# Attention and mixture-of-experts layer: in cross-only steps TensorE turns probabilities before x, and the output projection stands ahead of q

## What is computed

```python
def _L0_xattn_ref(queries, keys, values, Wq, bq, Wk, bk, Wv, bv, Wo, bo):
    q = (queries @ Wq + bq).reshape(B, L, H, dk)
    k = (keys @ Wk + bk).reshape(B, S, H, dk)
    v = (values @ Wv + bv).reshape(B, S, H, dk)
    scores = jnp.einsum('blhd,bshd->bhls', q, k)
    scores = jnp.where(causal[None, None], -jnp.inf, scores)
    attn = jax.nn.softmax(scores * scale, axis=-1)
    out = jnp.einsum('bhls,bshd->blhd', attn, v).reshape(B, L, H * dk)
    return out @ Wo + bo

x = x + _L0_xattn_ref(_layernorm(x, axis=-1), ctx_1024, ctx_1024, ...)
x = x + _L0_ffn_ref(_layernorm(x, axis=-1), ...)
```

## Time and profile before

| What | us |
|---|---|
| Median of three executions | 1707.7 |
| The profiled execution | 1707.36 |
| Its span | 1705.6 |
| Cross-only steps | 0 to 216 |
| Steps 14 to 51, routing, experts | 216 to the end |
| PE busy in the span | 1526.3 (89%) |
| DVE, ACT, POOL busy | 959.7, 688.9, 779.4 |
| xc load, median from issue to landing | 3.0 |

### The profile page before, as it was taken

How to read it: one execution, slowest core, us unless ns; L and a number is a source line. 1 busy time by engine, 2 the same in 40 slices (tenths; PEclk the granted TensorE clock), 3 DMA queues, 4 the chain that set the end, 5 groups by cost and what they waited for, 6 DMA issues and landing times. The chain is left out here.

```text
span 1705.6 us, 30593 instructions
## 1 busy us (share of the span) xinstructions
PE 1526.3 (89%) x11078; PEld 1332.6 (78%) x11079; DVE 959.7 (56%) x1691; ACT 688.9 (40%) x1359; POOL 779.4 (46%) x792
## 2 busy tenths in 40 slices
PE   4798888999999999999815899999999979999986
PEld 3566667888888888888714889899899869899975
DVE  2576555777777776777558535452333454443361
ACT  1234343555555555455320535343333444333341
POOL 1243334555555546565332546654343565463342
PEclk9999988999999999999958899999999989999999
DMA  6011121122122212111131334433332443342221
GB/s 233 22 56 51 63 70 43 63 71 74 66 71 66 79 58 69 68 64 61 48 110 36 90 68 93 101 94 87 71 91 39 99 111 81 79 106 59 35 39 22
DMA packets 62910, 124.09 MB, mean 73 GB/s; under 512 B 13456, under 2 KB 14128, under 8 KB 61865
## 3 DMA queue, kind: packets, MB, share of 16 engines
q1 hardware_dynamic: 44512, 92.41, 16.4%
q0 software_dynamic: 17920, 29.08, 9.8%
q10 hardware_dynamic: 328, 0.50, 0.1%
HBM read 88.69 MB, written 46.14 MB: 79 GB/s over the span
## 5 line engine op out<-in xcount | busy, mean ns | idle before, releaser
L1279 PE MATMUL hidden_ps<-gT,w 128*128 128x256 f32 x2880 | 352.4, 284 | 5.7 <-ACT hT L1201 2.2
L1279 PEld LDWEIGHTS hidden_ps<-gT,w 128*128 128x128 f32 x2880 | 350.0, 192 | 9.5 <-ACT hT L1201 4.9
L1308 PE MATMUL expert_ps<-w,hT 128*128 128x512 f32 x1440 | 340.6, 396 | 8.0 <-DVE og L1248 8.0
L1308 PEld LDWEIGHTS expert_ps<-w,hT 128*128 128x128 f32 x1440 | 272.6, 191 | 64.6 <-DVE og L1248 8.5
L1226 DVE TENSOR_TENSOR hT<-gl,hT 128x512 fp32r<-128x512 f32 x160 | 131.9, 833 | 247.4 <-ACT hT L1201 241.2
L1087 POOL TENSOR_TENSOR w<-raw,w 128x1024 fp32r<-128x1024 f32 x64 | 154.6, 2429 | 222.7 <-ACT w L1081 221.6
L1199 ACT ACTIVATE gl<-hidden_ps 128x512 f32<-128x512 f32 x160 | 95.6, 597 | 337.0 <-PE hidden_ps L1279 205.8
L1181 POOL DMA_INDIRECT out_dram<-og,idx x80 | 132.2, 1653 | 155.7 <-DVE og L1248 142.1
L1248 DVE TENSOR_SCALAR og<-expert_ps,shares 128x512 f32<-128x512 f32 x80 | 59.1, 749 | 162.6 <-PE expert_ps L1308 152.0
L1209 ACT ACTIVATE gT<-yk 128x256 fp32r<-128x256 f32 x160 | 66.9, 418 | 140.1 <-DVE yk L1235 138.1
L636 DVE TENSOR_TENSOR x<-main_ps,xc 128x512 f32<-128x512 f32 x32 | 22.1, 692 | 153.9 <-PE main_ps L315 153.9
(11 more groups left out here) (173 smaller groups left out, 3141.3 us busy)
## 6 DMA issues: line engine op xcount, KB each, us to landing
raw<-L_ffn_moe_w_dram SPq DMA_DIRECT2D x64, 512.0 KB
xa<-x_dram SPq DMA_DIRECT2D x32, 256.0 KB, 2.6
xc<-x_dram SPq DMA_DIRECT2D x32, 256.0 KB, 3.0
attended_rows<-x SPq DMA_DIRECT2D x32, 256.0 KB, 2.0
fx<-attended_rows SPq DMA_DIRECT2D x128, 64.0 KB
normed_tokens<-h SPq DMA_DIRECT2D x128, 64.0 KB
out_dram<-fx SPq DMA_DIRECT2D x128, 64.0 KB
fx<-qkv_rows_dram SPq DMA_DIRECT2D x1, 1536.0 KB, 6.4
```

The costliest lines, as they stand in the source:

```text
L1279: last = pe.matmul(pH[:, q, f * W:(f + 1) * W], w1[p][l][:, k, cols], xT[g.s % 2][r][:, k, :], start=k == 0 and n == 0, stop=k == KT - 1 a ...
L1308: last = pe.matmul(pY[:, k, :], hT[par][l][:, f, k * P:(k + 1) * P], w2[p][r][:, f, :], start=f == 0 and n == 0, stop=f == FT - 1 and n == 2)
```

## The change

In steps below FF TensorE turns the probabilities first, then x, then does the output projection, and q after it; psum_jobs lists them so; ScalarE copies xT_hi behind the four pT, and so in step 1 behind the token copies and wo_hi. From step 14 on the order is as before. VectorE, GpSimd and SyncE are not touched.

```diff
--- before.py
+++ after.py
@@ -158,10 +158,15 @@
     tx, tq, tp, tw = tile(i, 1), tile(i, 2), tile(i, LP), tile(i, LP + 1)
     fz, fq, fs, fo, ft, fr = (tile(i, FF + n) for n in range(6))
     free = 1 if i < FF else 0
-    jobs = [("xt", tx, 0, free)] + [("pt", tp, j, free) for j in range(4)] + [("p2t", fo, 0, 0), ("zt", fz, 0, 0)]
+    jobs = [("xt", tx, 0, free)] + [("pt", tp, j, free) for j in range(4)]
+    if free:
+        jobs = jobs[1:] + jobs[:1] + [("wo", tw, 0, free)]
+    jobs += [("p2t", fo, 0, 0), ("zt", fz, 0, 0)]
     if i % 2 == 0:
         jobs += [("q", tq, 0, 0), ("q", tq, 1, 0)]
-    jobs += [("wo", tw, 0, free), ("s2", fs, 0, 1), ("o2", fo, 0, 1), ("s", tq, 0, 0), ("qkv", fq, 0, 1),
+    if not free:
+        jobs += [("wo", tw, 0, free)]
+    jobs += [("s2", fs, 0, 1), ("o2", fo, 0, 1), ("s", tq, 0, 0), ("qkv", fq, 0, 1),
              ("lg", fr, 0, 1), ("qkv", fq, 1, 1)]
     if tq is not None and tq < S:
         jobs += [("val", tq, 0, 1)]
@@ -472,7 +477,7 @@
             act.activation(wq[0][:, :, :], rq, ACT.Copy).then_inc(s["wq_hi"], 1)
             for i in range(STEPS):
                 t = tile(i, 1)
-                if t is not None:
+                if t is not None and i >= FF:
                     act.wait_ge(s["xt_mm"], t + 1)
                     need(act, s["q_mm"], 2 * (t // 2))
                     act.activation(xT[0][:, :, (t % 2) * P:(t % 2 + 1) * P], parts(bank("xt", t)), ACT.Copy)\
@@ -491,6 +496,12 @@
                         act.activation(pT[:, j, :, :],
                                        bank("pt", t, j)[0:SK, :].rearrange("p (g n) -> p g n", g=4),
                                        ACT.Copy).then_inc(s["pt_evac"], 1)
+                t = tile(i, 1)
+                if t is not None and i < FF:
+                    act.wait_ge(s["xt_mm"], t + 1)
+                    need(act, s["q_mm"], 2 * (t // 2))
+                    act.activation(xT[0][:, :, (t % 2) * P:(t % 2 + 1) * P], parts(bank("xt", t)), ACT.Copy)\
+                        .then_inc(s["xt_hi"], 1)
                 f = tile(i, FF + 3)
                 if f is not None:
                     act.wait_ge(s["p2t_mm"], f + 1)
@@ -734,6 +745,25 @@
                     last = pe.transpose(bank(kind, t)[:, k * P:(k + 1) * P], src[:, k * P:(k + 1) * P], ident)
                 return last
 
+            def turn_x(tx):
+                pe.wait_ge(s["normed_x"], tx + 1)
+                transposes("xt", tx, xa[:, tx % 3, :]).then_inc(s["xt_mm"], 1)
+
+            def turn_probabilities(tp):
+                for b in range(4):
+                    pe.wait_ge(s["shared"], 2 * tp + b // 2 + 1)
+                    bank_free(pe, "pt", tp, b)
+                    for g in range(4):
+                        last = pe.transpose(bank("pt", tp, b)[0:SK, g * P:(g + 1) * P], pr[:, tp % 2, b, g, :],
+                                            ident)
+                    last.then_inc(s["pt_mm"], 1)
+
+            def project_out(tw):
+                pe.wait_ge(s["o_lo"], tw + 1)
+                bank_free(pe, "wo", tw)
+                split_matmuls(pe, bank("wo", tw), lambda h, k: oT[h][:, k, :], lambda h, k: wo[h][:, k, :])\
+                    .then_inc(s["wo_mm"], 1)
+
             pe.wait_ge(ctx_in, 16)
             pe.wait_ge(wk_in, 16)
             for n in range(8):
@@ -746,17 +776,14 @@
             for i in range(STEPS):
                 tx, tq, tp, tw = tile(i, 1), tile(i, 2), tile(i, LP), tile(i, LP + 1)
                 fz, fq, fs, fo, ft, fr = (tile(i, FF + n) for n in range(6))
-                if tx is not None:
-                    pe.wait_ge(s["normed_x"], tx + 1)
-                    transposes("xt", tx, xa[:, tx % 3, :]).then_inc(s["xt_mm"], 1)
+                if tx is not None and i >= FF:
+                    turn_x(tx)
                 if tp is not None:
-                    for b in range(4):
-                        pe.wait_ge(s["shared"], 2 * tp + b // 2 + 1)
-                        bank_free(pe, "pt", tp, b)
-                        for g in range(4):
-                            last = pe.transpose(bank("pt", tp, b)[0:SK, g * P:(g + 1) * P], pr[:, tp % 2, b, g, :],
-                                                ident)
-                        last.then_inc(s["pt_mm"], 1)
+                    turn_probabilities(tp)
+                if tx is not None and i < FF:
+                    turn_x(tx)
+                if tw is not None and i < FF:
+                    project_out(tw)
                 if fo is not None:
                     pe.wait_ge(s["shared2"], fo + 1)
                     transposes("p2t", fo, p2.rearrange("p b k -> p (b k)")).then_inc(s["p2t_mm"], 1)
@@ -773,11 +800,8 @@
                             last = split_matmuls(pe, bank("q", tq, j)[:, m * 256:(m + 1) * 256],
                                                  lambda h, k: wq[h][:, k, cols], lambda h, k: xT[h][:, k, :])
                         last.then_inc(s["q_mm"], 1)
-                if tw is not None:
-                    pe.wait_ge(s["o_lo"], tw + 1)
-                    bank_free(pe, "wo", tw)
-                    split_matmuls(pe, bank("wo", tw), lambda h, k: oT[h][:, k, :], lambda h, k: wo[h][:, k, :])\
-                        .then_inc(s["wo_mm"], 1)
+                if tw is not None and i >= FF:
+                    project_out(tw)
                 if fs is not None:
                     pe.wait_ge(s["q_turned"], fs + 1)
                     pe.wait_ge(s["k_turned"], fs + 1)
```

## The result

The changed kernel takes **1722.1 us** (median of 4 runs, 1719.5 to 1724.9) against 1708.3 (4 runs of the kernel before beside it): a ratio of 1.008, 95% interval 1.0062 to 1.0098. It is slower by 13.8 us; the forecast was 1718.0, in a range of 1710 to 1723.

A forecast was written before the change was run, and what follows sets the result against it. It took VectorE to bound odd steps and TensorE even steps in the first 216 us. Terms -5.5 + 1.45 + 6.7 + 3.7 + 2.6 + 1.9 = +10.8 on the kernel before gave 1718 us, range 1710 to 1723.

The forecast's parts named there:

- (a): Start, step 1: wo_hi no longer waits behind tile 0's transpose copy; tile 1's norm and all after gain 5.5 us.
- The collision: Start: VectorE's wq_lo and GpSimd's wo_lo meet at 22.7 us; if wo_lo waits it ends near 29, price 0.
- (b): Step 4: xT_hi waits behind four pT copies, q starts at 72.8 instead of 71.34: +1.45 us, perhaps 0.8 more.
- (c): Odd steps 5 to 13: xT_hi 2.22 us late delays VectorE's chain to mask: +6.7 us, +3.7 in 11 and 13.
- (d): Even steps 6 to 12: the copy of q, no longer covered by wo, delays the scores: +2.6 us together.
- (e): TensorE's clock in even steps: longer idle time brings two slow episodes of four, +1.9 us; range none to 7.2.
- rival B: Slower still: a low clock in every even step and a longer one in step 4; 1724 us, chance 0.09.
- A: Faster: ScalarE's order costs nothing, odd steps end on TensorE, the mask following scores, not norm_x; 1699 us, chance 0.11.
- C: About even: the odd steps' delay is half the forecast's, with no slow clock; 1711 us, chance 0.07.
- D: The start does not gain because wo_hi waits for something later than the landing at 20.6; 1724 us, chance 0.03.

The follow-up runs named there:

- version 1: The kernel before with only ScalarE's copy of tile 0's transpose moved behind wo_hi in step 1: 1706.6 us, ratio 0.9987.
- version 3: The changed kernel with q ahead of the output projection again, the rest as changed: 1728.4 us, ratio 1.0122.
- version 4: The changed kernel with filler matmuls in TensorE's idle stretch at the head of steps 6, 8, 10 and 12: 1714.1 us, ratio 1.0034.
- version 5: version 1 with VectorE's norm_x moved behind the subtraction of the row maxima in steps 1 to 13: 1698.3 us, ratio 0.993.
- version 2: version 1 with the output projection ahead of q in cross-only steps, x still turned first: 1708.7 us, ratio 0.9999.
- version 6: The changed kernel with xT_lo behind the exponential sums and statistics of x in steps 5, 7, 9, 11 and 13: 1705.9 us, ratio 0.9974.
- version 7: version 6 with norm_x also moved behind the subtraction of the row maxima in steps 1 to 13: 1699.3 us, ratio 0.9935.
- version 11: The kernel before with only norm_x moved behind the subtraction of the row maxima in steps 1 to 13: 1704.0 us, ratio 0.9987.

## Why the prediction came out as it did

**(a) The start, right.** -5.07 against -5.5, by the path described; counted from the start of wq_lo, which came 0.34 us later in this execution (22.63 against 22.29), it is -5.41. I took nothing for the clock at the start; q to scores took 8.31 us instead of 8.68 there, 0.37 back. The collision was seen; I had wo_lo end "near 29" if it had to wait, and it ended at 29.3. The Trainium skill, "SBUF — State Buffer", section "SBUF: two separate sides", has the port pair as an exclusive lock held by the first to start; wo_lo's 6.17 us beside an undisturbed wq_lo of 2.28 agrees. Waiting wq_lo out (1.78 us, to 24.91) and then taking 4.50 would make 6.28. The other order occurred too: in versions 1, 3, 4 and 5 wo_lo started first, kept 4.5 us, and it was wq_lo that took 6.1 to 6.4; in version 2 the two started within 0.02 us of each other and wq_lo kept its time. In version 1:

```profile
22.44 4.52 POOL L416 TENSOR_TENSOR wo_lo<-pr,wo_hi 128x2048 fp32r<-128x2048 f32 x1 [8.07 <-ACT wo_hi L485]
```

```profile
22.71 6.40 DVE L602 TENSOR_TENSOR wq_lo<-fx,wq_hi 128x2048 fp32r<-128x2048 f32 x1
```

The price is 0 either way: the first q comes 14.55 us behind wq_lo's start in the changed kernel and 14.54 in version 1.

**(b) Step 4, right in size, half for another reason.** +1.47 against +1.45. Locally q came only 0.71 later (71.34 - 5.07 to 66.98); the other 0.76 is q to scores at a low clock (8.61 us instead of 7.85), which I had named as an "up to 0.8 more" and not counted. Version 1, which has only the start, is slow for longer in step 4 as well (9.18 us).

**(c) Odd steps, right.** 1.92 us each against 2.22 in steps 5, 7 and 9, and 2.45 and 2.50 against 1.84 and 1.85 in 11 and 13: +10.7 against +10.4, of which 0.5 in each of 11 and 13 is not there in version 4. I put that down to the clock; in step 11 its slow stretch is shorter there (184 to 188 us against 183 to 190), for step 13 it is not shown. The 2.22 was 0.3 too large because I took the four copies at the 2.24 us of the earlier trace rows, where the fourth waited for its quarter. With all quarters turned in time xT_hi starts 1.91 us after the first copy. Version 6 shows the chain by taking its head away; version 2, whose steps 5, 7 and 9 do not change, shows that wo's place has no part in it.

**(d) Even steps at full clock, right.** +0.51, +0.56, +0.57 and +1.20 in version 4, against 0.52, 0.57, 0.50 and 0.98. The bare copy of q is worth 1.14 to 1.22 by version 2; half of it comes back because the last quarter no longer waits for xT_lo.

**(e) The clock, mis-sized.** This is the one term that failed. I took two episodes of four at 0.96, +1.9; measured were four of four, 7.0 us in steps 6 to 12. In steps 6, 8, 10 and 12 the last quarter to the scores took 12.01, 11.57, 13.07 and 13.13 us, where the forecast's own sum at full clock (0.78 + 2.89 + 6.89 from step 12's) is 10.6. I gave "2.81 us of idle time in step 12 did not bring it down" as evidence against. That gap was the exception of four: in the same trace the gaps of 3.53 us in step 4 and of 2.68 in steps 11 and 13 were followed by 0.50. I had the slow wo of 11 and 13 in part (c) and the slow step 4 in part (b), and drew nothing from them for the clock. The gaps then became 3.18 and 5.73, as I had worked out myself ("about 3", "near 4.7").

So what happened is rival B's mechanism (1724, with a chance of 0.09 that was too low): a low clock in all four even steps and a longer one in step 4. That the time still fell inside my range is in part luck. I had written that what the first 216 us lose is carried to the end; 2.7 us came back late, in the drain. With them the profiled execution would have stood at 1724.4, above the 1723 where I had ended the range. What comes back is not a constant either: version 4 is 10.0 us late at step 13 and 5.2 in its span.

Sum as measured: -5.1 + 1.5 + 10.7 + 2.8 + 7.0 - 2.7 = +14.2, the profiled difference (1721.7 - 1707.4 = 14.3).

Of the rivals, A fell on its own deciding point: the mask follows norm_x, 3.6 us behind the scores. Yet version 7 has what A asked for, in the changed order: once xT_lo and norm_x are out of the way, the odd step ends on TensorE. That it also took the 1699 us that A gave is a coincidence; A's sum has other terms. C and D did not occur.

## What to carry to other kernels

When work is put second on one engine, look at who holds a place in line for its result: here the reordering cost 1.9 us in each odd step only because VectorE's subtraction, not needed before the next step, stood ahead of sums that were. Move that and norm_x too, and the same order beats the kernel before by 0.65%. But compare with the right kernel: the order of before, given the same start and the same late norm_x, beats it by 0.70%. The gain was in the start and in norm_x, not in the new order. Filler that kept TensorE's clock up paid only while there was idle time to fill: it gave 8 us in the changed kernel and cost 8 in the version without the gaps, so remove the wait first.

## What the runs showed that I had not expected

An idle stretch on TensorE can cost more than itself. In the changed kernel the gaps of 3.2 us ahead of the third quarter in step 6 and of 5.7 ahead of the last in step 12 came with a granted clock of 0.50, while in version 6 a gap of 0.90 in step 6 did not: 7.0 us of slow matmuls in four even steps. The length of the gap does not decide alone: in the kernel before 2.68 us brought it and 2.81 did not, and in version 1 the clock fell in step 8 behind gaps of 0.60, 0.73 and 0.37 us.

An edit's gain can come and go with the clock. Version 1 moves everything 5.0 us forward and changes nothing else, and lost 1.33 us in step 4, where the stretch at 0.50 is longer than in the kernel before, and 1.59 in step 8, where the kernel before has none. Not even changed code is needed for it: up to step 4 version 6 is the changed kernel, and yet that step took 19.75 us in its profiled execution and 18.93 in the changed kernel's, with the slow stretch at 62 to 73 us instead of 60.5 to 71. Added to version 11 by version 5, the same start kept 5.07. The rows do not show what brings such a stretch on in the one case and not in the other; that stays open.
